# The last group of a second feed-forward tile by tile, and float32 fillers in routing

## What is computed

```
h = patch tokens joined with text
h = h + attention(layernorm(h))
h = h + experts(layernorm(h))             # 8 small experts and a shared one
h = h + linear_attention_block(layernorm(h))
h = h + routed_experts(layernorm(h))      # 8 experts, two per row

def linear_attention_block(x):
    ctx = ...                             # linear attention over elu(q), elu(k), v
    a = layernorm(ctx @ Wo + bo + x, g1, be1)
    f = gelu(a @ W1 + b1)
    return layernorm(f @ W2 + b2 + a, g2, be2)

def routed_experts(x):
    probs = softmax(x @ router_w.T)
    the two largest per row, normed to sum 1, weigh
    gelu(x @ w1[e].T + b1[e]) @ w2[e].T + b2[e]
```

## Time and profile before

| | us |
|---|---|
| runs before | 1013.37, 1014.4, 1017.34 |
| profiled execution | 1013.4 |
| its span, first to last instruction | 1011.2 |
| mean granted clock of TensorE | 0.964 |
| TensorE busy | 929.5 (92%) |
| VectorE busy | 573.3 (57%) |
| ScalarE busy | 589.2 (58%) |
| POOL busy | 632.9 (63%) |

### The profile page before, as it was taken

The page is one execution under the profiler, slowest core; times in us unless marked ns, Lnnn a source line. Parts: engine busy times, 40 slices in busy tenths (PEclk is TensorE's granted clock), DMA queues, the critical chain, the costliest instruction groups (busy, mean ns, idle before and its releaser), DMA issues. The chain is left out here.

```text
span 1011.2 us, 21243 instructions
## 1 busy us (share of the span) xinstructions
PE 929.5 (92%) x6856; PEld 852.5 (84%) x6856; DVE 573.3 (57%) x1327; ACT 589.2 (58%) x1243; POOL 632.9 (63%) x632
## 2 busy tenths in 40 slices
PE   6997999998899999799889999978999999999990
PEld 5885777777899988699879999878999999999990
DVE  1547999985766665688445666571333333333334
ACT  0342777775566664777445566322766667666644
POOL 3574888876555554443289987502787777778760
PEclk9999999999999999899999999967999999999995
DMA  8773444431211110000260000443566666666657
GB/s 309 251 257 87 138 157 157 157 137 52 96 64 64 52 74 2 1 2 1 84 259 1 17 17 32 173 192 106 157 207 201 190 189 199 207 198 193 187 185 274
DMA packets 66776, 134.62 MB, mean 133 GB/s; under 512 B 12809, under 2 KB 29364, under 8 KB 65524
## 3 DMA queue, kind: packets, MB, share of 16 engines
q1 hardware_dynamic: 58126, 116.49, 34.4%
q0 software_dynamic: 4032, 11.02, 3.0%
q10 hardware_dynamic: 4550, 6.24, 1.8%
HBM read 111.56 MB, written 23.21 MB: 133 GB/s over the span
## 5 line engine op out<-in xcount | busy, mean ns | idle before, releaser
L122 DVE CAST place<-place 128x512 fp32r<-128x512 f32 (+1 forms) x168 | 88.3, 568 | 156.0 <-PE moe_down L128 87.9
L2540 POOL TENSOR_TENSOR place<-place,place 128x512 fp32r<-128x512 f32 x84 | 138.1, 1644 | 50.1 <-DVE place L122 44.5
L2566 PE MATMUL moe_up<-place,place 128*128 128x128 f32 x1344 | 157.0, 275 | 0.5 <-ACT place L2665 0.5
L2566 PEld LDWEIGHTS moe_up<-place,place 128*128 128x128 f32 x1344 | 153.4, 192 | 0.8 <-ACT place L2665 0.8
L128 PE MATMUL moe_down<-place,place 128*128 128x256 f32 x1008 | 132.4, 288 | 4.0 <-DMA place<-w_remainder 2.2
L128 PEld LDWEIGHTS moe_down<-place,place 128*128 128x128 f32 x1008 | 124.6, 193 | 4.6 <-issue 4.6
L128 PE MATMUL ff_up<-place,place 128*128 128x384 f32 (+2 forms) x540 | 111.1, 349 | 0.8 <-issue 0.7
L2682 ACT ACTIVATE place<-moe_up,place 128x128 f32<-128x128 f32 x336 | 95.3, 367 | 16.8 <-POOL place L2540 12.5
L2669 ACT ACTIVATE place<-place 128x2048 f32 x42 | 80.3, 1915 | 31.7 <-PEq L2320 18.6
L128 PEld LDWEIGHTS ff_up<-place,place 128*128 128x128 f32 x540 | 90.8, 196 | 5.1 <-issue 0.9
L1779 POOL TENSOR_TENSOR place<-place,place 128x384 fp32r<-128x384 f32 x42 | 44.1, 1052 | 67.0 <-ACT place L1584 45.2
(11 more groups left out here) (315 smaller groups left out, 1966.8 us busy)
## 6 DMA issues: line engine op xcount, KB each, us to landing
place<-w_remainder SPq DMA_DIRECT2D x168, 256.0 KB
place<-in_w_dram SPq DMA_DIRECT2D x4, 4096.0 KB, 13.5
place<-gate_rows SPq DMA_DIRECT2D x24, 384.0 KB, 4.8
place<-in_w_dram SPq DMA_DIRECT2D x16, 512.0 KB, 3.4
w_remainder<-place SPq DMA_DIRECT2D x16, 512.0 KB, 2.9
place<-choices SPq DMA_DIRECT2D x5, 768.0 KB, 6.7
place<-value_rows SPq DMA_DIRECT2D x56, 64.0 KB, 2.2
place<-in_patches_dram SPq DMA_DIRECT2D x8, 384.0 KB, 5.3
```

The source lines that it names most:

```text
L122: return eng.tensor_copy(out, x)
L2540: pool.tensor_tensor(lo[f], raw[f], hi[f].bitcast(F32), ALU.subtract).then_inc(h_split, 1)
L2566: last = pe.matmul(p1[u][k // HK][:, (k % HK) * P:(k % HK + 1) * P], ws[u][:, c, k * P:(k + 1) * P], xT[u][:, c, :], start=(c == 0), stop= ...
```

## The change

In `second_feed` the last group is no longer worked as one. VectorE applies the gain, adds to h and takes statistics tile by tile in a written order that mixes the three tiles; the first gain waits for one normed tile only. TensorE does its fillers first, writing them to bank 3 of `up` instead of bank 0, turns each tile as soon as it is normed into its own bank of `up`, and makes its router products when its copy is out; the single filler between turn and products of the last group is gone. The copies of the turned tiles move from ScalarE to VectorE, between `pick` of the group before and `pick` of the last. In `route_second` the fillers become float32 of 256 columns, 20 and 2 of them where there were 90 and 8 of fp32r with 128 columns, and the cast of their operand goes.

```diff
@@ second_feed, TensorE
+                def flip_tile(j):
+                    a = NT - G + j
+                    pe.wait_ge(unit[5], a + 1)
+                    for c in range(C):
+                        last = pe.transpose(up[:, j, c * P:(c + 1) * P], x[:, a, c * P:(c + 1) * P], self.ident)
+                    last.then_inc(tile_turned, 1)
+
+                def logits_of_tile(j):
+                    if j == 0:
+                        pe.wait_ge(lg_read, NG - 1)
+                    pe.wait_ge(zt_tile, j + 1)
+                    for c in range(C):
+                        last = pe.matmul(turn[:, 0, GW + j * E:GW + (j + 1) * E], zt[(NG - 1) % 2][:, c, j * P:(j + 1) * P], self.router[:, c, :],
+                                         start=(c == 0), stop=(c == C - 1))
+                    if j == G - 1:
+                        last.then_inc(lg_mm, 1)
@@
-                for g in (NG - 2, NG - 1):
-                    busy(up[:, 0, :], 6 if g == NG - 2 else 16)
-                    flip_out(g)
-                    busy(up[:, 0, :], 1)
-                    logits(g)
+                busy(up[:, 3, :], 6)
+                flip_out(NG - 2)
+                busy(up[:, 3, :], 1)
+                logits(NG - 2)
+                busy(up[:, 3, :], 16)
+                for j in range(G):
+                    flip_tile(j)
+                for j in range(G):
+                    logits_of_tile(j)
@@ second_feed, VectorE
+                def gain_tile(j):
+                    a = NT - G + j
+                    dve.wait_ge(unit[4], a + 1)
+                    dve.tensor_tensor(x[:, a, :], x[:, a, :], self.g2, ALU.mult).then_inc(gained2, 1)
+
+                def add_h_tile(j):
+                    a = NT - G + j
+                    dve.wait_ge(gained2, NG + j)
+                    dve.wait_ge(be2_added, NT)
+                    dve.tensor_tensor(h[:, a, :], h[:, a, :], x[:, a, :], ALU.add).then_inc(h_added, 1)
+
+                def stats_tile(j):
+                    dve.wait_ge(h_added, NG + j)
+                    dve.bn_stats(stats[5][:, j, :], h[:, NT - G + j, :]).then_inc(counted[5], 1)
+
+                def copy_tile(j):
+                    dve.wait_ge(tile_turned, j + 1)
+                    dve.tensor_copy(zt[(NG - 1) % 2][:, :, j * P:(j + 1) * P], up[:, j, 0:C * P].rearrange("p (c s) -> p c s", c=C)).then_inc(zt_tile, 1)
+
                 add_down(NG - 1)
                 moments_down(NG - 1)
-                add_h(NG - 1)
+                gain_tile(0)
+                gain_tile(1)
+                add_h_tile(0)
+                stats_tile(0)
+                add_h_tile(1)
+                gain_tile(2)
+                stats_tile(1)
+                add_h_tile(2)
+                stats_tile(2)
+                for j in range(G):
+                    dve.wait_ge(counted[5], NT - G + j + 1)
+                    dve.bn_aggr(mv[5][(NG - 1) % 2][:, j, :], stats[5][:, j, :]).then_inc(moments_done[5], 1)
                 pick(NG - 2)
+                for j in range(G):
+                    copy_tile(j)
                 pick(NG - 1)
@@ second_feed, ScalarE
-                copy_out(NG - 1)
                 copy_logits(NG - 1)
@@ route_second
-                dve.tensor_copy(unit_rows, self.ident).then_inc(unit_cut, 1)
@@
-                pe.wait_ge(unit_cut, 1)
                 for k in range(2):
-                    keep_busy(pe, idle, unit_rows, unit_rows, 90 if k == 0 else 8)
+                    keep_busy(pe, idle, self.ident, self.h[:, 0, :], 20 if k == 0 else 2)
```

More of the change, by code:

```diff
@@ L1897, in second_feed @@
         self.xn_rows = self.dram("xn_rows", [NT * P, D])
+        tile_turned, zt_tile = sem("sf_tile_turned"), sem("sf_zt_tile")
         biased, weights_cut, f1_split, f2_split = sem("sf_bo_added"), sem("sf_weights_cut"), sem("sf_f1_split"), sem("sf_f2_split")
@@ L2312, in route_second @@
         spare = m.take(8)
-        unit_rows, unit_cut = m.take_rounded(P), sem("route2_unit_rows")
         consts = self.route_consts
```

## The result

| | us |
|---|---|
| changed kernel, median of 4 runs | 1003.87 (1003.09 to 1006.24) |
| kernel before, median of 4 runs | 1015.71 (1013.37 to 1017.34) |
| ratio of the two | 0.9891, 95% interval 0.986 to 0.9923 |
| profiled execution of the changed kernel, its span | 1003.09, 1001.0 |

The forecast was 1001.4 with 999.0 to 1006.0, and over 0.5% faster. The gain by medians is 11.8 us; by spans it is 1011.2 - 1001.0 = 10.2.

A forecast was written before the change was run, and what follows sets the result against it. Three serial chains ahead of the fixed-rate expert loop were taken as the bound: last group, routing, expert opening. Gains 2.0 + 9.2 + 1.3 = 12.5 us off 1013.4 give 1000.9, named 1001.4 between two bases, range 999.0 to 1006.0.

The forecast's parts named there:

- The sum: Whole kernel: gains of 2.0, 9.2 and 1.3 us add to 12.5, off the profiled execution's 1013.4 us.
- Part 1: Last group worked tile by tile: logits read at about 659.55 against 661.58, 2.0 us gained.
- by a hair: Last group: TensorE's 16 fillers end at 656.6, just meeting the first normed tile, at a cost of 0.1 us at most.
- Part 2: Routing: shorter fillers let the slot table be read at 682.2 us against 691.43, 9.2 us gained.
- the rise c: Routing: time from first filler to the clock's rise, taken as 4.1 us; below 6.4 the second hot map comes last.
- Part 3: Opening of the expert stage: 1.8 us gained if the clock holds, 0.3 to 1.0 with a dip; taken as 1.3.
- no lift: Rival in routing: new fillers do not raise the clock, 40 records end at 684.6, total 1009.3 us; chance 0.12.
- the next to be late is ScalarE's copy, which waits for the biases: Expert opening, clock held: copy starts 5.1 us after the start, first product at 5.55, 1.8 us gained.
- The case with a dip: Expert opening: a clock dip makes the ten fillers take 5.6 to 6.3 us, gain 0.3 to 1.0 us.
- The dip over the opening: Clock falls at TensorE's gaps, about as likely as holding; rival where it stays down into the opening: 1002.7 us, 0.12.
- The clock that stays low in the expert loop: Rival: clock falls and holds low into the expert loop, up to 6.7 us more a block, 1021 us; chance 0.02.
- the tile-wise tail does nothing: Rival in the last group: nine operations at 0.44 us and a late copy leave 0 to 1.4 us; chance 0.07.

The follow-up runs named there:

- e1: Changed kernel with the old routing fillers (90 and 8 of fp32r, 128 columns) and their cast back, so only the tile-by-tile last group is new; ratio to before 0.999.
- e4: Changed kernel with no fillers in routing, the ten of the expert stage kept; one execution, table read 21.01 us after the logits.
- e3: Changed kernel with half of the old fp32r 128-column fillers in routing, 45 and 4, and their cast; ratio to before 0.9907.
- e2: Kernel before with only the new routing fillers (20 and 2 of float32, 256 columns), without the cast, last group worked as before; ratio to before 0.9901.
- e9: The changed kernel itself measured again, beside the other runs on the same chip; 1005.69 us, ratio to before 0.9891.
- e11: Changed kernel with gain, addition and statistics of the last group as one group again; one execution, logits 10.20 us after the first norm.
- e10: Changed kernel with 10 fillers instead of 16 ahead of the last group's turns; ratio to before 0.9887.
- e7: Changed kernel with biases and remainders requested after the first gather, ScalarE's copy before the second staging, 6 opening fillers instead of 10; ratio to before 0.9875.
- e8: Changed kernel with biases requested after the gather, copy before second staging, 6 opening fillers, 10 tail fillers, 4 before the second table product; 1002.67 us, ratio to before 0.9844.
- e5: Changed kernel with routing fillers of float32, 128 columns, 40 and 4 of them; one execution, table read 20.59 us after the logits.
- e6: Changed kernel with routing fillers of fp32r, 256 columns, 45 and 4, both operands cast; one execution, table read 20.95 us after the logits.

## Why the prediction was right

The sum was 12.5 us and the stages between the same marks show 12.3. Its base, "a profiled execution", was the loose end: the same code ahead of the change was 2.04 us slower in the second profile, so the spans show 10.2 and the medians, which average over that, 11.8.

- **Part 1**, 2.0 forecast, 2.22 measured. The aggregates end 4.33 us after the first norm (4.3 forecast), POOL and the norm keep 1.96, the turns meet the normed tiles, the products start with the third turn's end as laid out. The 0.2 more are the products, 1.40 us where 1.55 was laid out. The remark that the fillers meet the first tile "by a hair" was the important one, and I drew the wrong size from it: I priced it at 0.1 us, and with a dip of the clock under the fillers it costs 2 us (e1, e4). That the profile of the change had none there was luck, if the likelier case: six of the eight profiles had none.
- **Part 2**, 9.2 forecast, 9.28 measured; fillers 10.76 us for 10.65, products of the table 0.87 for 1.0, table read behind VectorE's last work, as stated. The clock rose 3.8 us after the first filler (4.1 forecast). By the text's own terms the second hot map comes last as long as the rise c stays below 6.0 us (677.9 + c/2 against 680.94), not 6.4; with 3.8 nothing hung on it. But the text tied this part to the clock, and e3 and e4 show that it hardly hangs on it: 0.4 us. The rival "no lift" was not refuted as a price, because 20 float32 calls at 0.50 would indeed hold the queue for 17 us; no run of them stayed down. In the six other profiles with those fillers it rose as well.
- **Part 3**, 1.3 forecast, 0.81 measured, with the clock at 1.00 throughout, for which 1.8 was given. The step that failed is "the next to be late is ScalarE's copy, which waits for the biases". The biases did land 4.98 us after the start; but the gathered rows landed at 5.5, and the turn and the copy stand behind them in series. The waits of the profile before do not show the gather, since the fillers covered it until 6.4. That cover was the thing taken away, and I named only one of the two transfers beneath it. That the clock held was not the usual case (see below); with the dip the step does not matter, for then the fillers are last again. The case with a dip (0.3 to 1.0 forecast) gave its low end, 0.3 to 0.4, in e2, e9 and e11 (7.00, 7.00 and 6.94 us for 7.33), and was missed in e10.
- **The rivals.** The dip over the opening came in four of the five profiles of changed or near-changed kernels that keep all ten fillers and the new routing ones (e2, e9, e10, e11, not the first), and in both with six fillers (e7, e8), more often than the even chance I gave it. e10 even fell short of before, 8.27 us from start to product: its clock fell at 683.3, before the opening began, and rose at 690.1. The clock that stays low in the expert loop was not seen: the rest is 310.6 to 312.8 us everywhere, the longest in e5 with a dip from 691.3 to 694.7 at its start. Its price had a slip: two cold blocks at 6.7 us are 13.4 and already eat the 12.5. That the tile-wise tail does nothing was one of the rivals, and in e1 it nearly came true, by another mechanism than the one named.

The Trainium skill, TensorE: Matmul & The Clock Gate, section "Part 1: The HAM clock gate", says that sustained activity releases the clock. By that rule the old fillers should have lifted it. The runs side with the trace of before: fp32r products of 128 columns kept the engine busy for 9.8 and 19.4 us at 0.50.

## What to carry to other kernels

Filler work that stands in a queue ahead of a real step is part of that step's path: size it by what its slowest clock makes of it, against the moment at which the data of the step behind it are ready, and look at whether the filler lifts the clock at all. When a cover is taken away (fillers here), list every transfer and every step beneath it, for the profile shows only the last of them. Small stage gains are read from marks within the trace, for here the same code ahead of them moved by 5 us from one execution to the next.

## What the runs showed of the hardware

- Fillers of fp32r with 128 columns did not raise the granted clock in 19.4 us; fp32r with 256 columns, float32 with 128 and float32 with 256 did, within 1.8 to 4.6 us of their start in routing (the two kinds of e5 and e6 in one profile each); in the opening it rose up to 6.0 us after the first of the float32 fillers (e10).
- The clock falls in short dips, and not all at the same places in executions of the same code (at 485 us in the profile before, not in e9). Up to the first norm of the last group, two profiles:

```profile
0.00:649.70 649.70, 605.29 (x4179) 532.50 (x4180) 429.30 (x1015) 380.70 (x779) 408.88 (x458) 0.99 0.28 97
```
```profile
0.00:654.70 654.70, 611.49 (x4179) 537.32 (x4180) 430.17 (x1015) 380.35 (x779) 406.50 (x458) 0.98 0.29 97
```

The first is before, the second e2_routing_only; the same 4179 records took TensorE 6 us more at a mean clock lower by 0.01. From the first rise up to 640 us the traces' clock record adds up to 13.7 us at 0.50 in the first and 23.9 in the second, which could make most of their 5. But dips alone do not order all the executions: e6 has 23.9 us at 0.50 and its norm at 651.02, e9 has 20.5 and 653.56. What else moves them is open.
- A dip is not always as short as the 3.4 us of rows 7: the one under the last group's fillers lasted 6.8 us in e1, e2, e4 and e8, with TensorE busy in them.
- A gather of 128 rows landed 4.8 us after its issue began beside 1 MB of biases and the first remainders, and 3.0 us when neither had been asked for yet (e7).
